# A three-part transformer decoder layer: initial loads reordered, exponential's table loaded ahead, a normalisation split in two, new step order

## What is computed

```python
x = layernorm(x + attn(x, W1, W2, W3, W4))      # one head: softmax(x W1 (x W2)^T / 16) (x W3) W4
# second sublayer, inside: cross attention to ctx (375 rows, 16 heads of 16), self attention (16 heads),
# feed-forward 256 -> 1024 (gelu) -> 256; each with residual, layernorm, gain and shift
x = layernorm(x + xattn(x, ctx, mask, ...))
# third: each token picks 1 of 8 experts by its largest score with the centroids
expert = argmax(feats @ centroids.T)
y = feats + relu(norm(feats) @ W1e.T + b1e) @ W2e.T + b2e
x = layernorm(x + alpha * y + (1 - alpha) * feats)   # alpha = sigmoid(feats . centroids[expert])
```

## Time and profile before

| | us |
|---|---|
| median of 3 runs | 400.49 (400.34 to 400.58) |
| the profiled execution, its own time | 399.32 |
| its span, first to last instruction | 397.6 |
| PE busy | 383.7 |
| DVE / ACT / POOL busy | 268.1 / 236.3 / 130.3 |

### The profile page before, as it was taken

One profiled execution on the slowest core, in us unless ns is written; L12 is line 12 of the kernel. 1 busy time (PEld: TensorE's weight loads), 2 busy tenths in 40 slices (PEclk: granted clock), 3 DMA queues, 4 the chain that ended last, 5 costly groups with the idle time before them and its releaser, 6 DMA issues.

```text
span 397.6 us, 10377 instructions
## 1 busy us (share of the span) xinstructions
PE 383.7 (97%) x3696; PEld 325.8 (82%) x3696; DVE 268.1 (67%) x931; ACT 236.3 (59%) x808; POOL 130.3 (33%) x258
## 2 busy tenths in 40 slices
PE   7999999999999999999999999999989999999992
PEld 7876887987878878788888898887978998999671
DVE  5377857887678676696886843768868776434431
ACT  1114958778898888989999975685411232332230
POOL 5242212422115041032321311544173636751321
PEclk9999999999999999999999999999999999999998
DMA  6963180430010100600000000991195234499300
GB/s 203 285 143 134 39 213 33 166 105 2 17 43 19 40 2 19 252 0 20 2 2 3 2 2 2 377 430 42 26 398 248 63 123 120 143 397 422 135 15 32
DMA packets 11415, 46.93 MB, mean 118 GB/s; under 512 B 1552, under 2 KB 6128, under 8 KB 9200
## 3 DMA queue, kind: packets, MB, share of 16 engines
q1 hardware_dynamic: 8896, 31.79, 23.0%
q0 software_dynamic: 1920, 12.35, 8.0%
q10 hardware_dynamic: 544, 2.08, 1.8%
HBM read 41.31 MB, written 4.91 MB: 116 GB/s over the span
## 4 chain that ended last, share of the span: by engine, by line
PE 91%; DVE 4%; POOL 2%; issue 2%; ACT 0%; POOLq 0%; DVEq 0%; ACTq 0%
PE bank_pt L648 15%; PE bank_out L489 12%; PE bank_scores L504 7%; PE bank_out L515 7%; PE bank_out L670 7%; PE bank_scores L632 7%; PE bank_out L475 5%; PE bank_pt L683 5%; PE bank_out L693 5%; PE bank_out L482 5%; PE bank_out L544 3%; PE bank_scores L638 2%; PE bank_out L496 1%; PE bank_pt L576 1%; PE bank_out L586 1%
## 5 line engine op out<-in xcount | busy, mean ns | idle before, releaser
L1244 ACT ACTIVATE arena<-arena,negmaxc 112x375 f32<-112x375 f32 x128 | 77.3, 608 | 12.0 <-DVE negmaxc L989 11.7
L989 DVE CUSTOM_DVE_ANT_0 arena<-bank_scores,arena 112x375 f32<-112x375 f32 x128 | 65.5, 541 | 18.0 <-PE bank_scores L638 13.7
L1264 ACT ACTIVATE arena<-bank_pt 125x448 f32<-125x448 f32 (+1 forms) x128 | 66.1, 546 | 18.9 <-PE bank_pt L648 17.9
L648 PE MATMUL bank_pt<-ident,arena 112*125 112x112 f32 (+1 forms) x512 | 70.6, 272 | 0.0
L648 PEld LDWEIGHTS bank_pt<-ident,arena 112*125 112x125 f32 (+1 forms) x512 | 62.5, 175 | 9.2 <-issue 1.4
L489 PE MATMUL bank_out<-arena 128*112 128x256 f32 (+1 forms) x224 | 57.3, 383 | 0.0
L1255 ACT ACTIVATE arena<-bank_scores,negmaxs 112x112 f32<-112x112 f32 x128 | 43.4, 355 | 4.4 <-DVE negmaxs L995 4.1
L489 PEld LDWEIGHTS bank_out<-arena 128*112 128x112 f32 (+1 forms) x224 | 37.2, 182 | 5.9 <-issue 0.6
L1300 ACT ACTIVATE arena<-bank_scores,consts 128x128 f32<-128x128 f32 x64 | 18.2, 368 | 39.4 <-PE bank_scores L504 39.4
L1355 POOL TENSOR_TENSOR vareps<-meanvar,scal 112x1 f32<-112x1 f32 (+1 forms) x49 | 10.2, 207 | 89.0 <-DVE meanvar L865 80.2
L504 PE MATMUL bank_scores<-arena 128*128 128x128 f32 x256 | 30.4, 277 | 0.9 <-DVE arena L1161 0.9
(11 more groups left out here) (189 smaller groups left out, 688.0 us busy)
## 6 DMA issues: line engine op xcount, KB each, us to landing
arena<-moe SPq DMA_DIRECT2D x8, 2048.0 KB, 13.2
arena<-ctxT SPq DMA_DIRECT2D x8, 375.0 KB, 3.4
arena<-mask SPq DMA_DIRECT2D x8, 164.1 KB, 3.0
x_slots<-arena SPq DMA_DIRECT2D x8, 130.0 KB, 3.1
arena<-x_slots SPq DMA_DIRECT2D x8, 130.0 KB, 2.3
arena<-weights SPq DMA_DIRECT2D x1, 1024.0 KB, 5.5
arena<-fi SPq DMA_DIRECT2D x1, 1024.0 KB, 5.7
arena<-fo SPq DMA_DIRECT2D x1, 1024.0 KB, 8.4
```

The source lines that it names most:

```text
L648: last = nc.tensor.transpose(dst[0:kp, j * S:(j + 1) * S], probs[0:S, (n % 2) * HG + j, c * kp:(c + 1) * kp], ident[0:S, 0:S])
L989: v.tensor_tensor_reduce(out=probsC[0:S, i % (2 * HG)], in0=score_bank[j][0:S, 0:KX], in1=masks[0:S, u % 2], scale=-1.0, scalar=3.0e38, op ...
L1244: a.activation(probsC[0:S, i % (2 * HG)], probsC[0:S, i % (2 * HG)], ACT.Exp, bias=negmax["c"][0:S, u, at:at + 1], scale=-1.0, accum_out=s ...
L1264: a.activation(probsT[0:kp, n % RT, c], pt_bank[PT[stage, i] % RP][0:kp, 0:HG * S], ACT.Copy).then_inc(pt_free, 1)
```

## The change

Five things:

1. **First loads.** W1 is issued by ACT at once; SP issues all else. x of batches 2 and 3 stands ahead of W3 and W4, the cross key and value weights ahead of the context, the cross query weights (256 KB) and the second halves of other loads behind. Two loads are split in two and get semaphores of their own.
2. **Table.** ACT computes one column's exponential as soon as the identity exists, so that the table of the exponential is loaded there.
3. **Normalisation.** The first of `zf`'s two operations moves to the end of `f2`, behind its statistics and ahead of the wait for POOL's 1/deviation.
4. **Fillers.** They become a step `wm` of 4 products that the order places: five such steps, 20 products where there were 24.
5. **Order.** The whole string is new.

```diff
-WARM = {("sc", 6): 8, ("rk", 6): 6, ("zx", 7): 6, ("ei", 0): 4}
+WARM = 4
 WARM_FIRST = 6
 ORDER = (
-    "aqk as aqk at aw as av aqk at av as ay ck ay as at av*2 ab at ay aqk ab ck as ax as av cq ck qk at cm*3 cv cm ck ax cm qk ct cm ct "
+    "aqk*2 as aqk at aw as av*2 at ay as ck av as ab ay at aqk ck av as ax as ay cq at ck qk cm*3 at cm cv ck qk cm*2 ab av cv ct cm ax "
...
-    "rk zb zf f1 room rk zn f1 al zb zn zx f2 sc zf rk zx en zb zn sc al ei al rk first*4 tot first*4 ")
+    "room rk f1 zb zn zx f2 sc zf wm*3 al wm en zx rk zb sc zn wm ei rk first*2 tot first*3 al first*3 ")
...
+        table_loaded = sb("table_loaded", [128, 1])
...
             sp.dma_start(xT_sb[:, 0:1], xT[:, 0:1]).then_inc(x_first_in, 16)
-            sp.dma_start(wA[:, 0:1], weights[:, 0:1]).then_inc(w_first, 16)
             sp.dma_start(wA[:, 1:2], weights[:, 1:2]).then_inc(w_second, 16)
             sp.dma_start(consts[:, :], cols).then_inc(consts_in, 16)
             sp.dma_start(xT_sb[:, 1:2], xT[:, 1:2]).then_inc(x_second_in, 16)
+            sp.dma_start(xT_sb[:, 2:4], xT[:, 2:4]).then_inc(x_early_in, 16)
             sp.dma_start(wA[:, 2:4], weights[:, 2:4]).then_inc(w_third, 16)
-            sp.dma_start(xT_sb[:, 2:4], xT[:, 2:4]).then_inc(x_early_in, 16)
             sp.dma_start(R["b4"], rows[:, 0:D].to_broadcast([S, D])).then_inc(b4_in, 16)
-            sp.dma_start(resid[0:S, 0:4], xrow[:, 0:4]).then_inc(xrow_first_in, 16)
...
+            sp.dma_start(resid[0:S, 0:2], xrow[:, 0:2]).then_inc(xrow_first_in, 16)
+            sp.dma_start(wC[:, 1:3], weights[:, 5:7]).then_inc(w_cross, 16)
+            sp.dma_start(context[:, 0], ctxT[0]).then_inc(ctx_in[0], 16)
+            sp.dma_start(v_bias[:, 0], vb[0:1].to_broadcast([128, D])).then_inc(v_bias_in, 16)
+            sp.dma_start(resid[0:S, 2:4], xrow[:, 2:4]).then_inc(xrow_second_in, 16)
+            sp.dma_start(R["cob"], rows[:, D:2 * D].to_broadcast([S, D])).then_inc(cob_in, 16)
+            sp.dma_start(wC[:, 0:1], weights[:, 4:5]).then_inc(w_query, 16)
+            sp.dma_start(masks[0:S, 0], mask[0:1].to_broadcast([S, KX])).then_inc(mask_in[0], 16)
+            sp.dma_start(context[:, 1], ctxT[1]).then_inc(ctx_in[1], 16)
+            sp.dma_start(xT_sb[:, 4:8], xT[:, 4:8]).then_inc(x_late_in, 16)
...
-                for n in range(WARM.get((stage, i), 0)):
-                    if n == 0:
+                elif stage == "wm":
+                    if i == 0:
                         pe.wait_ge(probs_ready, PROBS["sm", GROUPS - 1] + HG)
-                    mm(bank[0][:, 0:128], ident[:, :], ident[:, :], start=True, stop=True)
+                    for n in range(WARM):
+                        mm(bank[0][:, 0:128], ident[:, :], ident[:, :], start=True, stop=True)
...
                     take_stats(k)
+                    if stage == "f2":
+                        dve.wait_ge(stats_ready, k + 1)
+                        link(v.scalar_tensor_tensor(ybuf[0:S, k % NR], ybuf[0:S, k % NR], meanvar[0:S, k % NR, 0:1], R["fog"],
+                                                    ALU.subtract, ALU.mult))
+                        centred[i] = chain[0]
...
                     k = open_norm(stage, i)
-                    link(v.scalar_tensor_tensor(ybuf[0:S, kf % NR], ybuf[0:S, kf % NR], meanvar[0:S, kf % NR, 0:1], R["fog"],
-                                                ALU.subtract, ALU.mult))
-                    linked()
+                    dve.wait_ge(dve_chain, centred[i])
...
-            act.wait_ge(w_first, 16)
-            act.dma_start(wC[:, 0:3], weights[:, 4:7]).then_inc(w_cross, 16)
...
+            act.dma_start(wA[:, 0:1], weights[:, 0:1]).then_inc(w_first, 16)
+            act.wait_ge(setup, 1)
+            a.activation(table_loaded[:, :], ident[:, 0:1], ACT.Exp)
```

39 lines of the change are left out of this document (18 added, 21 removed), and 26 rows, old and new, of the table ORDER.

## The result

| | before | after |
|---|---|---|
| median of 4 executions each, side by side, us | 400.53 (400.34 to 400.68) | 394.85 (394.68 to 394.92) |
| ratio, 95% interval | | 0.9867 (0.9850 to 0.9885) |
| profiled execution / its span, us | 399.32 / 397.6 | 394.81 / 393.1 |

Both profiled executions together give only 4.5. So there are two differences to explain: 1.3 us by which the spans differ more than forecast, and 1.2 us that the profiled executions don't show.

The account below looks back on a forecast made before the run. PE was taken to bound the kernel (busy 383.7 of 397.6 us). Start -1.1, middle 0, 290 to 302 -1.6, ranking -0.4 and expert part -0.1 sum to -3.2: median from 400.5 to 397.3, range 395.6 to 399.7.

Parts of the forecast that it names:

- Start: First 20 us: waits at the first `as` and `at` go and W1 comes earlier; -1.1 us, between -1.6 and +0.5.
- Both waits: PE's waits at the first `as` (for DVE's key copy) and first `at` (for ACT's exponential); 0.48 us each to go.
- The -0.1 for W1: First loads: W1 on ACT's queue goes out sooner; gain between 0 and 0.2, loss at most 1.5, taken as -0.1.
- 290 to 302: Gaps behind `f1` pieces 12 and 13 (1.13 + 0.43) go; -1.6 us, between -1.9 and -0.5.
- Ranking: From 313.6 to 322 us: DVE's chain counts; `zn` 7 leaves (0.56), `al` 6 comes in (0.15); -0.4 us.
- Expert part: Its first wait, 0.91 at 330.51 us, barely changes and the rest stays; -0.1 us, up to +0.5.
- Middle: From 20 to 290 us: PE idle only 0.26 of 270 us, so no gain; 0, from -0.5 to +2.5.
- The step from profile to median: Whole run: the profiled execution lay 1.2 us below the median, so forecast 396.1 profiled became a median of 397.3.
- A: Between 20 and 290 us the new order, tight on ACT, costs PE 1 to 2.5 us; 399.0; chance 0.24, shared with another rival.
- C: Cross heads' scores and masks: middle costs more than all else gives; 401.5 at 0.13 us a group; chance 0.09.
- B: More gain: wait ahead of `aw` (0.5), half that between the `sc`, short waits hidden in the middle; 395.8; chance 0.08.
- D: PE's clock halves after pausing about 0.8 us ahead of the last `rk`, with fewer fillers; 401.1; chance 0.04.

## Why the prediction was wrong

**Start, -1.1: right.** 1.11 by the profiles, whose change of pace came at the same moment. Both waits went, the table was rightly counted once, `aw`'s wait stayed (0.52). The -0.1 for W1 did not come: PE left the fillers at 4.38 instead of 4.30. W1 did land earlier on ACT's queue, at 4.08 instead of 4.26; but x of the first batch, which had landed at 2.90, now landed at 4.25, and PE needs both. So the 0 was met by a load that the prediction left out. The Trainium skill ("DMA: Bandwidth & Descriptors", "Queues, rings and completion order") says that each DMA engine takes turns between the queues that have work for it, and the landings agree: beside W1 on the other queue x took 3.5 us from its issue instead of 2.1. x of batches 4 to 7 landed at 21.6 (10.82 + 10.8) for a want at 22.22, later than the 19 to 20 forecast, since the core moved 248 GB/s in the first 20 us and not what before's rows gave for the second half (285): no wait here, but 0.6 us of slack where I had 2 to 3, and a wait in two other kernels with these loads.

**290 to 302, -1.6: right,** 1.61, each link as described, and the wait between the two `sc` (0.34) stayed.

**Ranking, -0.4: nearly,** 0.30. **Expert part, -0.1:** +0.18 up to tile 1, and 0 to the end.

**Middle, 0: the mis-sized term of the sum.** It measured -1.7 (-1.5 with the second profile of after), outside of its own bounds (-0.5 to +2.5). The step that failed is the sentence that PE was idle 0.26 of 270 us, "so nothing can be won but waits shorter than the modelled ends show": it names the right thing and then gives it nearly no room. Some 360 spacings between PE's steps lie behind it, and 20 to 100 ns at some of them are over a microsecond. Shown by runs: with the operation late, the new order gains 0.9, and the moved operation 0.6 to 0.8 on top, 0.5 of it at two steps from 257 us on, and not from 290. In the old order the moved operation would have cost 0.7, so the prediction missed an interplay of two of its own changes.

What the 1.7 consists of, the traces tell. Take for each kind of step, and for each way in which its neighbours use the array (in one piece, `qk`, `pv`), the shortest time to the next start in fifteen profiles as its time without a wait. So counted, the steps of the middle take 263.1 us in before and 262.2 in after: 0.9 us is in what stands next to what, of which the three entries fewer are an estimated 0.5. The other 0.8 are late starts, 4.2 us of them in before and 3.4 in after. The five largest of before are 0.29, 0.18, 0.17, 0.11 and 0.10 us; the first profile of after has none above 0.10, the second has one of 0.18. No run tests them one by one. This is the largest: the scores of `qk` 20 wait for ACT to have read the ones before, which it has at 153.86.

```profile
153.63 0.23 ACT L1255 ACTIVATION_READ_ACCUMULATOR arena<-bank_scores,negmaxs 112x1 f32 x1
...
153.96 0.58 PE L632 MATMUL bank_scores<-arena 32*112 32x375 f32 x4 [0.22 <-issue]
```

**The step from profile to median, 1.2 us: failed.** "It lay 1.2 below the median of the runs" was true of before and was carried over as if it were an overhead of the profile. It was chance: an execution with an early change of pace (5.4 us), set against a median of three without a profile. That these three changed later is likely, not shown; the profiled execution of before that took 400.46 changed at 7.6. After's profile differs from its median by 0.04. With all executions, before is at 400.1 and after at 395.1, which makes the difference 5.0 rather than 5.7.

**Rivals.** A and C, with the middle as a loss, were on the wrong side, and had 0.33 of the chance between them. B had the right sign and 0.08; of its three reasons the short waits hidden in the middle were real, and the waits ahead of `aw` and between the `sc` stayed. D did not come in after and came in two kernels one edit away from it.

## What to carry to other kernels

An engine that a view of windows shows as full for 270 us can still have 1 to 2 us in spacings of 20 to 300 ns: compare the starts of equal steps before giving such a stretch a 0. Read a load's landing against the moment at which the old and the new order want it; a new order and what goes with it are one change: the order alone and all the rest alone gave at most 0.5 us each, both together 5, and one moved operation costs 0.7 in one order and gains as much in another. And set a profiled execution against the spread of the timed ones before carrying their difference over.
